# Another order of the 208 steps of the mixer and cross-attention phase of a decoder layer

## The reference, cut to what matters

```python
x = x + attn(layernorm(x))                       # gated delta rule, 4 heads of 64, chunks of 32
x = x + xattn(layernorm(x), ctx_1024, mask)      # cross-attention, 16 heads of 16
x = x + ffn(layernorm(x))                        # fake-quantised gate, up and down projections

# attn, after convolutions and the delta rule:
stats  = cat([head_stats(t) for t in (local_short, local_long, delta_out, v_direct)])   # mean, var, |x|, l2
p      = softmax((gelu(cat([h, stats]) @ Wg1 + bg1) @ Wg2 + bg2) / softplus(temp)), floored and renormalised
o      = p0*local_short + p1*local_long + p2*delta_out + p3*v_direct + static*res_gate*local_short
og     = sigmoid(gelu(cat([h, head_stats(o), head_stats(v_direct)]) @ Wog1 + bog1) @ Wog2 + bog2)
out    = rmsnorm(o * og) @ Wo
```

## Time and profile before

| | |
|---|---|
| runs | 1268.60, 1270.09, 1273.96 us |
| profiled execution: own time, span | 1273.96 us, 1272.2 us |
| TensorE matmul busy, share of the span | 1071.3 us, 84% |
| TensorE weight loads | 806.0 us, 63% |
| VectorE, ScalarE, GpSimd | 986.7 (78%), 749.2 (59%), 641.7 us (50%) |
| phases a and b | about 0 to 287 us |
| phase cx, turns 0 to 5 | 287.3 to 520.8 us |
| turns 6 to 15 | 520.8 to 965.8 us, 44.5 us each |
| turns 16 to 22 | 965.8 to about 1155 us |
| phase f | to 1272.2 us |

### The profile page before, as it was taken

How to read it: one execution, slowest core, us unless ns; L and a number is a source line. 1 busy time by engine, 2 the same in 40 slices (tenths; PEclk the granted TensorE clock), 3 DMA queues, 4 the chain that set the end, 5 groups by cost and what they waited for, 6 DMA issues and landing times. The chain is left out here.

```text
span 1272.2 us, 27987 instructions
## 1 busy us (share of the span) xinstructions
PE 1071.3 (84%) x8552; PEld 806.0 (63%) x8626; DVE 986.7 (78%) x2955; ACT 749.2 (59%) x1456; POOL 641.7 (50%) x2360
## 2 busy tenths in 40 slices
PE   5888988684677789999999999999999987875755
PEld 4767766683556567777777777777777645443224
DVE  4989988685766869788888888888888776834985
ACT  5877877432343435675666567566656544444766
POOL 4777775405334744565566556556655654101007
PEclk9988889895557869999999999999999998997989
DMA  6667666546021434353353445335343442205007
GB/s 183 214 199 231 197 208 204 180 90 173 34 84 50 121 88 127 105 150 114 93 151 110 132 123 157 115 94 150 109 138 85 145 103 59 76 26 190 1 1 232
DMA packets 159829, 160.31 MB, mean 126 GB/s; under 512 B 65320, under 2 KB 126656, under 8 KB 159680
## 3 DMA queue, kind: packets, MB, share of 16 engines
q1 hardware_dynamic: 155552, 157.47, 41.7%
q10 hardware_dynamic: 4128, 1.05, 0.4%
HBM read 96.34 MB, written 61.87 MB: 124 GB/s over the span
## 5 line engine op out<-in xcount | busy, mean ns | idle before, releaser
L2142 DVE CUSTOM_DVE_ANT_0 x_psA<-x_psA,x_mask_q 128x256 f32<-128x256 f32 x496 | 201.1, 447 | 82.5 <-PE x_psA L1431 59.2
L1694 ACT ACTIVATE x_PT<-x_psB 128x512 f32<-128x512 f32 x240 | 143.2, 596 | 140.8 <-PE x_psB L1458 133.8
L314 DVE SCALAR_TENSOR_TENSOR a_conv<-a_ps_proj,taps,a_conv 128x253 f32<-128x253 f32 (+2 forms) x288 | 114.9, 470 | 12.5 <-ACT a_conv L381 12.5
L537 PE MATMUL a_ps_proj<-a_hT,wqkv 128*128 128x256 f32 x384 | 104.8, 421 | 11.0 <-DVE a_conv L314 7.8
L1431 PE MATMUL x_psA<-x_Ks,x_Qs 96*128 96x256 bf16 x496 | 97.8, 279 | 13.0 <-DVE x_maxima L2142 12.8
L1458 PE MATMUL x_psB<-x_Qs,x_Ks 98*128 98x256 bf16 x480 | 92.7, 274 | 7.3 <-ACT x_PT L1694 2.5
L537 PEld LDWEIGHTS a_ps_proj<-a_hT,wqkv 128*128 128x128 f32 x384 | 77.1, 212 | 30.2 <-issue 15.9
L2142 DVE DVE_READ_ACCUMULATOR2_ANT x_maxima<- 128x1 f32 x512 | 72.2, 141 | 0.0
L1455 PE MATMUL x_psB<-x_mask_k,x_ident_bf 128*128 128x512 bf16 x167 | 64.8, 388 | 8.5 <-ACT x_PT L1694 7.5
L1472 PE MATMUL x_psO<-x_PT,x_V 128*32 128x256 f32 x1024 | 70.3, 393 | 1.6 <-ACT x_PT L1694 1.6
L1431 PEld LDWEIGHTS x_psA<-x_Ks,x_Qs 96*128 96x128 bf16 x496 | 41.4, 101 | 47.0 <-DVE x_maxima L2142 26.8
(11 more groups left out here) (383 smaller groups left out, 3262.5 us busy)
## 6 DMA issues: line engine op xcount, KB each, us to landing
scratch_keypack<-a_keypack SPq DMA_DIRECT2D x16, 768.0 KB, 4.2
c_keypack<-scratch_keypack SPq DMA_DIRECT2D x16, 768.0 KB, 4.9
x_Ks<-scratch_k_parts SPq DMA_DIRECT2D x192, 64.0 KB, 2.7
matrix<-scratch_taps_copies SPq DMA_DIRECT2D x32, 256.0 KB, 4.0
scratch_k_parts<-x_parts_k SPq DMA_DIRECT2D x32, 192.0 KB, 2.3
scratch_q_parts<-x_parts_q SPq DMA_DIRECT2D x32, 192.0 KB, 2.3
x_Qs<-scratch_q_parts SPq DMA_DIRECT2D x32, 192.0 KB, 3.0
a_x_in<-in_x SPq DMA_DIRECT2D x16, 256.0 KB, 3.9
```

The costliest lines, as they stand in the source:

```text
L314: nc.vector.scalar_tensor_tensor(acc, ps_proj[PROJ_BANK[p]][:, c, 0:L - j], taps[:, p, c, TAPS - 1 - j:TAPS - j], acc, ALU.mult, ALU.add). ...
L537: last = nc.tensor.matmul(ps_proj[PROJ_BANK[p]][:, o], wqkv[:, p, c, o * P:(o + 1) * P], hT[par][:, c], start=c == 0, stop=c == FC - 1)
L1694: nc.scalar.activation(PT[:, k % (2 * GROUP)], bank_B(b, k)[0], ACT.Exp, scale=XD ** -0.5).then_inc(pexp_ready, 1)
L2142: last = nc.vector.tensor_tensor_reduce(bank_A(b, k)[0][:, s], bank_A(b, k)[0][:, s], mask_q[:, t], 1.0, LOWEST, ALU.add, ALU.max, maxima[ ...
```

## The change

The table `C_ORDER` is replaced. Both tables hold the same 208 names; 41 of them get another stage, and nearly all get another place. No branch of `part` is changed, no instruction of cx is added or taken out, and all waits stay as they are. The diff, cut to its first lines (the rows of the table tell a reader little):

```diff
--- before.py
+++ after.py
@@ -786,30 +786,30 @@
 
 
...
-C_ORDER = [(2, "rv"), (3, "osum3"), (4, "scale"), (5, "mA10"), (2, "delta"), (1, "invx"), (5, "mA11"), (1, "invq"),
...
+C_ORDER = [(0, "tt"), (3, "og2"), (3, "oge"), (1, "rv"), (3, "ogs"), (3, "ctxT"), (2, "tT"), (2, "tTc"), (3, "cTc"),
...
```

More of the change, by code:

```diff
@@ L784 @@
 NVB = 2
-C_ORDER = [(2, "rv"), (3, "osum3"), (4, "scale"), (5, "mA10"), (2, "delta"), (1, "invx"), (5, "mA11"), (1, "invq"),
-           (1, "att0"), (4, "oF"), (4, "klow"), (4, "rstdx"), (7, "rstdb"), (4, "qlow"), (3, "ostat"), (5, "mA12"),
[10 rows of a table removed]
-           (3, "st_qp"), (2, "ld_x"), (3, "ld_Q0"), (2, "ld_c"), (1, "ld_hT"), (3, "statx"), (4, "mA5"), (2, "pr1"),
-           (2, "pr2"), (4, "mA6"), (2, "pr3"), (1, "r1"), (0, "invr"), (4, "mA7"), (3, "xnx"), (2, "mixa"), (4, "mA8"),
-           (2, "mixb"), (2, "mixc"), (2, "mix"), (3, "qrest"), (4, "mA9"), (2, "osum"), (5, "sB4"), (1, "c0"), (4, "sA6"),
[9 rows of a table removed]
+C_ORDER = [(0, "tt"), (3, "og2"), (3, "oge"), (1, "rv"), (3, "ogs"), (3, "ctxT"), (2, "tT"), (2, "tTc"), (3, "cTc"),
[23 rows of a table added]
 LOWEST = -3.0e38
```

## The result

Four runs of the changed kernel took 1300.58 to 1302.46 us, median 1302.3; the kernel before took 1272.0 us (median of 4) beside it. The ratio is 1.0235, with a 95% interval of 1.0205 to 1.0267: slower, by 30 us. The profiled run took 1304.4 us, its span is 1302.6 us. The forecast was 1299 us against the median, 1303 as own time. One run further down, of a2_osum3_qrest, took 1766 us in a slow state at a granted clock of 0.55, and that kernel's median is the one of its other three.

A forecast was written before the change was run, and what follows sets the result against it. TensorE, busy 43.96 of 44.50 us in a middle turn, was taken as the bound, so order could only add waits. 33 us over 13 turns less 4 gave +29: 1299 us against the median, range 1267 to 1317.

The forecast's parts named there:

- The sum: Whole kernel: 33 us lost in turns 5 to 17, 4 won in the first turns, +29 us in all.
- the first turns: Start of the phase: batch 0 starts sooner, part is given back behind inverse steps; -4.3 us, bounds -9 and +3.
- the drain: End of the phase: the same chains without stats; taken as no change.
- the forecast's own signs: Profile rows expected if right, among them oT8 waiting 1.5 to 2.5 us and turns about 47 us apart.
- The wait of `oT8`: Middle turn: mA11 ahead of osum3 delays ostat and st8, so TensorE waits at oT8; 1.9 us, from 1.2 to 2.6.
- The walk: Step times added from sA11 over mA11, osum3, ostat and st8 to oT8: 9.1 us, against 7.20 of TensorE's work.
- The wait of `sA1`: Late in a middle turn: the chain stats, st16, sh2, sums, mA0 ends late for sA1; 0.15 us, bounds 0 and 1.0.
- Smaller joints: Middle turn: tu1, xT and sB12 come closer to what feeds them; 0.5 us in all, bounds 0 and 1.5.
- The rival of absorbed waits: TensorE has slack that swallows the middle turns' waits, only the first turns' gain shows: 1261 us, chance 0.11.
- waits that add up: All joints at their upper ends, or a lower clock; 4.4 us a turn in 13 turns: 1323 us, chance 0.11.
- cancel the gain: osum3 comes in time; 0.3 us a turn, 4 in all, meets the first turns' -4: 1270 us, chance 0.12.

The follow-up runs named there:

- a2: The changed kernel with osum3 moved ahead of sA11 and mA11, and qrest ahead of sA10 and mA10: 1292.5 us (three runs), ratio to before 1.016.
- a1: The changed kernel with osum3 alone moved ahead of sA11 and mA11: 1298.3 us, ratio to before 1.019.
- c1: As a2, with p1 and w5 also moved ahead of sA15: 1286.5 us, ratio to before 1.012.
- c2: As c1, with sums3a also moved behind mA0: 1289.1 us, ratio to before 1.014.
- a3: The changed kernel with maxT and its sh1 moved from right behind p1 to behind vproj and vc: 1312.4 us, ratio to before 1.029.
- a4: The changed kernel with the moves of a2 and a3, and out and pv1 each put one sB step later: 1315.5 us, ratio to before 1.033.
- d2: The changed kernel with p1 and w5 alone moved ahead of sA15, osum3 and qrest left late: 1303.7 us (one run).
- b2: The kernel before with sq1 alone moved one stage later, to the start of the next turn ahead of tTc: 1279.7 us, ratio to before 1.001.
- b1: The kernel before with osum3 alone moved from ahead of mA10 to right behind it: 1285.1 us, ratio to before 1.010.
- c3: As c2, with xd one stage later behind sq1, osq behind eB9, and pv1 between sB11 and sA12: 1301.1 us, ratio to before 1.023.

## Why the prediction was right, point by point

*The sum.* The phase was forecast 29 us longer and is 28.2. The middle turn was forecast at 47.05 and is 46.88. The mechanism holds: same work, new waits at fixed points of TensorE's queue, in every turn. But how close the sum comes is in part luck. Inside the turn the waits were shared out otherwise, and outside it two errors cancel: the first turns won 8.0 us instead of 4.3, and the drain lost 4.7 that were put at nothing. One of the forecast's own signs failed as well: `oT8` was to wait 1.5 to 2.5 us and waits 0.82, and the longest wait of a turn, at `maxT`, is in none of its terms.

*The wait of `oT8`*, 1.9. The mechanism holds (a2 takes the wait away). The walk gave 9.1 us; the rows give 0.42, 0.73, 0.87, 6.37 and 0.32, in sum 8.71. The 0.4 too much is `st8`: the 6.35 us for `ostat` ran to the start of `stats`, and `st8` starts at that same time, so its wait was counted twice. TensorE's own work is 8.71 less the waits of 0.82, 0.47 and 0.16 within it, 7.26; forecast 7.20. Late by 1.45 instead of 1.9 then, of which 0.47 show at `sB12`. The cause named was half of it: `qlow` behind `qrest` and `mA10` was equally late (a1, a2). And the turns with this wait were counted from 5 on; turn 4 has `osum3` and `mA11` together too, and its `oT8` waited 1.9 us.

*The wait of `sA1`*, 0.15. Not there in the middle turns of the changed kernel, and not in a2, c1 or c2 either. Where `sA1` does wait (a3, a4), `sh2` waits for `sh1` behind `vc`, not for the end of `stats`. But the claim behind it, that GpSimd's work ties the early waits to a late one, was right at another place. I had priced `rstdb` ahead of `scale` at nothing; its rows stand in that chain from 844.17 to 848.28, and GpSimd ends `oF` 0.06 to 0.3 us ahead of `to`, where it had 2.0 us to spare before. What is taken from a wait elsewhere comes up there (in d2 0.18 of 0.95 is won). That `rstdb` behind `scale` would free it wasn't tried.

*Smaller joints*, 0.5. `tu1` and `xT` don't wait. The joints that do are `maxT` right behind `p1` with 0.95, which I missed altogether although `maxT` waits for `w5` in the code, and `ctxT` with 0.2. This is the term of the turn that was mis-sized, 0.5 for 1.15, and it fills what the two others had too much. So the turn's sum is closer than its parts deserve.

*The first turns*, -4.3: -8.0 to the start of turn 5. `a0` came 12.5 us after the start of the phase instead of 18.0, 5.5 sooner (forecast 5.4). `invr` ahead of `r1` cost 2.7 at `out` (31.1 against b2's 28.4; forecast 2.9). From `out` to `gate1` of batch 0 it is 18.0 us instead of 22.4, 4.4 won where I had 3.7 for `stats`. But `stats` itself is only 2.2 us shorter (8.7 us instead of 10.95); 2.5 are won between `out` and its start, and 0.4 are lost behind it. Behind `inve` `sA1` waits 2.7 us in turn 4 (1.9); the turn as a whole is 2.2 longer. The rest is turn 3, 3.1 us shorter, at a granted clock of 0.78 instead of 0.71, for which the forecast had no term; why it was shorter isn't shown.

*The drain*, 0. It costs 4.7 us, and turn 17 is 4.8 us longer, 2.5 above the middle turns' 2.4 (turn 16 is only 1.2 longer). In turn 17 there is no `out` between `sA11` and `oT8` any more to fill the time, and `oT8` waits longest:

```profile
1068.53 0.59 PE L1345 MATMUL c_ps_e<-ident,c_stats 128*8 128x128 f32 x2 [3.29 <-DVE c_stats L2065]
```

In the turns from 18 on the cause stays open: a2, without the wait of `oT8` in its middle turns, has 91.0 us there too.

*The rival of absorbed waits* falls: 1.0 us of wait in b1 made the turn 0.86 longer, in an order otherwise untouched, and the rest is a wait behind it that it covers. The rule of the Trainium skill that stood beside it ("Perfetto Trace Analysis", section "Identifying the Most-Contended Engine") would have left a quarter of the turn free, weight loads being busy for 33.45 of 44.50 us before; the runs show no such room for a wait. The rivals of waits that add up (1323) and that cancel the gain (1270) are off by 21 and 32 us.

## What to carry to other kernels

In a software pipeline whose main engine is busy for 99% of a turn, a new wait lengthens the turn by most of its length; look for it at every step that stands directly behind the producer of its bank or input in the new order, not only on the longest chain. When a wait is repaired, ask which neighbour it was hiding: in a3, a4, c3 and b2 the move brought out a new wait of 0.4 to 1.1 us, each time because an unwanted step (`vc`, `xd`, `OT0`, `sq1`) stood ahead of the wanted one in ScalarE's queue. And before a few microseconds at the start of a phase are credited, look whether the clock is at its lower level in the turns behind it.

## What the runs showed that was not expected

- Behind a wait of 1.1 us a dense step can be slow as well: `gate1` took 4.1 instead of 2.5 us, at a granted clock of 0.59, in every second middle turn of a3 and in two turns of a4, though all their turns have the wait. It did not in the middle turns of before, of after (waits up to 0.95 us, ahead of `maxT`) and of b1 (1.0 us, ahead of `oT8`). What decides it is open.
- The unchanged phases ahead of cx ended anywhere from 283.7 to 293.5 us in 14 profiles. A difference under 10 us between two profiled runs says nothing until the stretch is known in which it lies.
